# Attention heads loaded by four transfers per half instead of twelve, with a source that repeats, and a split spread over later steps of the rotated pass

## What is computed

```python
q, k, v = heads(x @ Wq + bq), heads(x @ Wk + bk), heads(x @ Wv + bv)   # 16 heads of 8
# second attention: q, k = rope(q), rope(k)
attn = softmax(q @ k.T / sqrt(8))          # 512 x 512 for each head
x = x + (attn @ v) @ Wo + bo
```

## Time and profile before

| | |
|---|---|
| median of 3 runs | 4861.33 us (4853.15 to 4867.28) |
| profiled execution: time, span | 4843.5 us, 4841.7 us |
| TensorE busy | 4504.4 us, 93% |
| VectorE (DVE) busy | 3527.2 us, 73% |
| ScalarE (ACT) busy | 2281.7 us, 47% |
| GpSimd (POOL) busy | 2492.3 us, 51% |
| transfers a_ks<-a_scr, a_qs<-a_scr | 96 of 192 KB, 288 of 64 KB |
| transfers a_scr<-a_parts | 48 of 256 KB |
| mean granted TensorE clock | 0.945 of full speed |

### The profile page before, as it was taken

How to read it: one execution, slowest core, us unless ns; L and a number is a source line. 1 busy time by engine, 2 the same in 40 slices (tenths; PEclk the granted TensorE clock), 3 DMA queues, 4 the chain that set the end, 5 groups by cost and what they waited for, 6 DMA issues and landing times. The chain is left out here.

```text
span 4841.7 us, 116672 instructions
## 1 busy us (share of the span) xinstructions
PE 4504.4 (93%) x46192; PEld 2659.9 (55%) x46384; DVE 3527.2 (73%) x3728; ACT 2281.7 (47%) x3395; POOL 2492.3 (51%) x3501
## 2 busy tenths in 40 slices
PE   5999889999999999999999999999999998588897
PEld 2333356666666666666666666666666665222223
DVE  5777467777778777778778777777777875477763
ACT  1666544444444444444444444444444443046663
POOL 1111166666666666666566666666666663212212
PEclk6999989999999999999999999999999998689998
DMA  3222122222222222222222223222222222122210
GB/s 71 57 54 55 54 62 59 52 60 70 66 60 60 53 73 70 54 59 62 75 59 61 59 57 84 56 56 63 54 67 63 57 56 65 34 54 54 53 29 20
DMA packets 181498, 281.71 MB, mean 58 GB/s; under 512 B 58080, under 2 KB 79840, under 8 KB 175456
## 3 DMA queue, kind: packets, MB, share of 16 engines
q1 hardware_dynamic: 153664, 241.45, 20.9%
q10 hardware_dynamic: 27648, 37.79, 3.5%
HBM read 61.70 MB, written 17.56 MB: 16 GB/s over the span
## 5 line engine op out<-in xcount | busy, mean ns | idle before, releaser
L1015 DVE SCALAR_TENSOR_TENSOR x<-l_r,l_qkvec,l_tab 128x1024 f32<-128x1024 f32 x768 | 936.4, 1279 | 25.3 <-ACT l_sq L925 23.3
L503 DVE TENSOR_REDUCE a_nmax<-a_pair 128x2 f32<-128x1024 f32 x512 | 609.3, 1221 | 261.1 <-PE a_pair L585 261.0
L428 ACT ACTIVATE a_pt<-a_st 128x512 f32<-128x512 f32 x1024 | 542.7, 605 | 282.0 <-PE a_st L569 276.6
L860 POOL TENSOR_TENSOR l_ntmp<-l_seed 128x32 f32<-128x32 f32 (+1 forms) x480 | 111.0, 231 | 773.4 <-ACT l_seed L914 754.6
L893 POOL TENSOR_TENSOR l_p<-l_p,l_srec 128x1024 f32<-128x1024 f32 x192 | 365.3, 1902 | 248.9 <-DVE l_srec L1094 192.5
L887 POOL TENSOR_TENSOR l_u<-x 128x512 f32<-128x512 f32 x384 | 490.7, 1278 | 0.0
L888 POOL TENSOR_TENSOR l_u<-x 128x512 f32<-128x512 f32 x384 | 489.9, 1276 | 0.0
L1264 PE MATMUL l_r<-l_pbd,l_va 128*64 128x160 f32 (+1 forms) x6144 | 442.7, 297 | 13.8 <-DMA l_pbd<-l_pt 13.5
L975 ACT ACTIVATE l_p<-l_p 128x1024 f32<-128x1024 f32 x192 | 203.5, 1060 | 520.3 <-DVE l_p L1073 520.3
L1174 PE MATMUL l_r<-xs,l_wqkv 128*128 (+1 forms) x768 | 424.1, 658 | 25.8 <-DVEq L1082 23.1
L1264 PEld LDWEIGHTS l_r<-l_pbd,l_va 128*64 128x64 f32 x6144 | 396.7, 138 | 74.9 <-issue 74.9
(11 more groups left out here) (179 smaller groups left out, 7385.3 us busy)
## 6 DMA issues: line engine op xcount, KB each, us to landing
l_kbd<-l_kn SPq DMA_DIRECT2D x1536, 64.0 KB, 2.0
l_pbd<-l_pt SPq DMA_DIRECT2D x768, 64.0 KB
l_pbd<-l_pt ACTq DMA_DIRECT2D x576, 64.0 KB
a_ks<-a_scr SPq DMA_DIRECT2D x96, 192.0 KB
a_qs<-a_scr SPq DMA_DIRECT2D x288, 64.0 KB
a_scr<-a_parts SPq DMA_DIRECT2D x48, 256.0 KB, 2.5
l_pbd<-l_pt SPq DMA_DIRECT2D x192, 56.0 KB
l_wqkv<-in_wqkv SPq DMA_DIRECT2D x6, 1536.0 KB, 6.9
```

Source lines behind the costliest of these rows:

```text
L428: nc.scalar.activation(pt[n % 2][:, r, :], st[(4 * n + r + par) % 3][:], ACT.Exp, scale=SC).then_inc(exp_done, 1)
L503: nc.vector.tensor_reduce(out=nmax[:, n, 2 * i:2 * i + 2], in_=pair[i][:], op=ALU.max, axis=AX.X, negate=True).then_inc(pair_dve[i], 1)
L1015: last = nc.vector.scalar_tensor_tensor(out=t[a][:, 2 * half:2 * half + 2, :], in0=R[a][:, half, :].unsqueeze(1).to_broadcast([D, 2, T]), ...
```

## The change

`load_heads` issues four transfers per half. The source of each begins with a dimension of three copies (step zero): one transfer fills all 72 rows of `ks`, and one for each part of q fills 24 rows of `qs`. The bytes written into `ks` and `qs` are the same. The wait at `qs_full` counts 4 transfers instead of 12. In the rotated pass the fourth and fifth piece of the split stand at steps 10 and 11 instead of 9 and 9.

```diff
                     h = slice(8 * half, 8 * half + 8)
+                    sp.dma_start(ks[p][0:KROWS, h, :],
+                                 scratch[p][1].rearrange("j (e h) t -> (j e) h t", e=HD)[:, h, :].unsqueeze(0)
+                                 .to_broadcast([SPLIT, SPLIT * HD, 8, T])).then_inc(qs_full[half], 16)
                     for i in range(SPLIT):
                         r = i * SPLIT * HD
-                        sp.dma_start(ks[p][r:r + SPLIT * HD, h, :],
-                                     scratch[p][1].rearrange("j (e h) t -> (j e) h t", e=HD)[:, h, :]).then_inc(qs_full[half], 16)
-                        for j in range(SPLIT):
-                            r = (i * SPLIT + j) * HD
-                            sp.dma_start(qs[p][r:r + HD, h, :],
-                                         scratch[p][0, i].rearrange("(e h) t -> e h t", e=HD)[:, h, :]).then_inc(qs_full[half], 16)
+                        sp.dma_start(qs[p][r:r + SPLIT * HD, h, :],
+                                     scratch[p][0, i].rearrange("(e h) t -> e h t", e=HD)[:, h, :].unsqueeze(0)
+                                     .to_broadcast([SPLIT, HD, 8, T])).then_inc(qs_full[half], 16)
...
-                split_slots = (4, 5, 6, 7, 8) if rope is None else (8, 8, 9, 9, 9)
+                split_slots = (4, 5, 6, 7, 8) if rope is None else (8, 8, 9, 10, 11)
...
-                            pe.wait_ge(qs_full[half], seen.next(qs_full[half], SPLIT * (SPLIT + 1) * 16))
+                            pe.wait_ge(qs_full[half], seen.next(qs_full[half], (SPLIT + 1) * 16))
```

## The result

The changed kernel takes 5003.35 us (median of 6 runs, 4983.91 to 5019.1) against 4846.92 us of the kernel before (6 runs, 4831.57 to 4867.28): a ratio of 1.0322, 95% interval 1.0297 to 1.0347. It is 156 us slower at the median; the profiled executions are 140.4 us apart (4843.5 and 4983.9 us, spans 4841.7 and 4982.1). The profiled execution of the changed kernel is the shortest of its six, so some 16 us of the difference at the median are in no trace. The forecast was 96 us more, 4957 us, with a range of 4865 to 5085 us.

What follows compares the result with a forecast made beforehand. TensorE, busy 93% of the span, was taken as the bound, with head loads barely hidden. Waits of 13.8 and 60.9 us plus 21 us of clock, together 96, on 4861.3 gave 4957 us, range 4865 to 5085.

Steps and rivals of the forecast that it cites:

- Three engines: Head loads: with three copies leading the source pattern, three DMA engines work, each with 48 rows instead of 15.
- The time of a row: Head loads: 0.32 us per 8 KB row on three engines, so a load takes 17.9 us, 3.5 longer than 14.3.
- Rival 1: Head loads: three engines but slow rows; 0.48 us gives 5079 us (chance 0.17), 0.79 us about 5430 us (0.04).
- rivals 2 and 3: Head loads on twelve engines: rival 2, rows at 0.79 us, 4870 us (0.12); rival 3, at 0.32 us, 4838 us (0.09).
- low end of three values: Row time with three engines: low 0.32 us from a sixteen-engine transfer, middle 0.48, high 0.79; the low was taken.
- Issuing hidden: SP's issue of head loads: twelve transfers take some 4 us, four about 1.4 us; the saving is hidden, costed at nothing.
- nothing to gain from the spread: Rotated pass, step 9: no TensorE stall behind the three pieces; the 2.77 us gap behind step 8 stays, so nothing gained.
- The waits: TensorE waiting for later loads in both attention passes: 13.8 us more in the plain pass, 60.9 in the rotated one.
- The later split: Rotated pass: the last split piece, and the scratch writes behind it, come 4.9 us later; 4.7 at the first boundary.
- The clock: Half clock after boundary stops: 3 us in each of six steady rotated units and once in the plain pass, 21 us.
- The sum: Whole kernel: plain pass 13.8, rotated pass 60.9 and clock 21 us, together 96 us, 2.0% slower.
- the forecast's own range: Three engines at about 0.32 us: 4925 to 4995 us, row at 0.31 to 0.36, clock's 21 us or none; chance 0.58.

Runs made afterwards that it cites:

- kernel with the copies second: Changed kernel with the three copies as second dimension of k's source, q's rows not repeated inside a transfer, split 8, 8, 9, 9, 9: 4840.28 us, ratio 0.9982.
- split alone: Kernel before, twelve transfers kept, rotated pass split at 8, 8, 9, 10, 11 instead of 8, 8, 9, 9, 9: 4925.53 us, ratio 1.0162.
- kernel with the copies second and the early spread: Four transfers with the copies as second dimension, rotated split at 7, 8, 9, 9, 9: 4835.78 us, ratio 0.9956; repeated, 4838.40 us, ratio 0.9964.
- transfers alone: Changed kernel with its four transfers but the earlier rotated split 8, 8, 9, 9, 9: 4935.84 us, ratio 1.0184.
- kernel with the copies second and the late steps: Four transfers with the copies as second dimension, rotated split at 8, 8, 9, 10, 11: 4882.12 us, ratio 1.0067.
- units shown above: Three units of the kernel with the copies as second dimension and rotated split 7, 8, 9, 10, 11: 4864.71 us, ratio 1.0012.
- Taking the pair apart: Kernel before, twelve transfers, rotated split at 7, 8, 9, 9, 9, so no two pieces stand together at step 8: 4863.62 us, ratio 1.0013.

## Why the prediction was right, and where its terms were off

**Three engines: right.** The share is 0.19 to 0.20, 79 to 80 GB/s. The kernel with the copies second shows the cause: it is the outermost count, not the repetition. The Trainium skill, "DMA: Bandwidth & Descriptors", rules for kernel authors, has this for a leading zero-stride dimension; the trace of the changed kernel agrees, with 0.19.

**The time of a row: the number right, its reason not shown.** 0.32 us taken, 0.32 measured; 17.9 us for a load, predicted 17.9. Rival 1 (0.48 us) fell with that, rivals 2 and 3 with the share. I had taken the low end of three values because each engine would write a run of partitions of its own. The same reasoning gave 0.35 us for the kernel with the copies second, and 0.55 came. So part of this hit is luck.

**Issuing hidden, nothing to gain from the spread: right.** The stop behind step 8 is 16.6 us in six units before and after. Fewer issues by themselves won nothing: with the copies second there are four as well, and that kernel is not clearly faster.

**The waits: nearly right in the rotated pass, too low in the plain one.** Predicted 13.8 us in the plain pass and 60.9 in the rotated one, measured 20.6 and 66.9. In the plain pass the row load came 4.2 us later, not 3.5, and at the boundary for which I had 1.3 us TensorE's stop grew by 2.4, from 0.91 to 3.27. In the rotated pass the first load (3.6 us longer against 3.5) and the first boundary (8.1 against 8.2) came out; the six steady boundaries have 9.9 us more each, or 9.2 less the waits for ACT, where I had 8.2.

**The later split: under-sized.** I took 4.9 us later for the scratch writes, from a stretch at full clock. DVE in the changed kernel, the steps 9 to 11:

```profile
4593.57 1.23 DVE L503 TENSOR_REDUCE a_nmax<-a_pair 128x2 f32<-128x1024 f32 x1 [0.70 <-PE a_pair L585]
4594.71 0.69 DVE L496 CAST a_parts<-a_left 128x1024 bf16<-128x1024 f32 x1
4595.49 1.23 DVE L503 TENSOR_REDUCE a_nmax<-a_pair 128x2 f32<-128x1024 f32 x1
4598.75 1.22 DVE L503 TENSOR_REDUCE a_nmax<-a_pair 128x2 f32<-128x1024 f32 x1 [2.04 <-PE a_pair L585]
4599.89 1.22 DVE L498 TENSOR_TENSOR a_left<-a_left,a_parts 128x1024 f32<-128x1024 f32 x1
4601.02 1.22 DVE L503 TENSOR_REDUCE a_nmax<-a_pair 128x2 f32<-128x1024 f32 x1
4604.08 1.22 DVE L503 TENSOR_REDUCE a_nmax<-a_pair 128x2 f32<-128x1024 f32 x1 [1.84 <-PE a_pair L585]
4605.23 0.68 DVE L496 CAST a_parts<-a_left 128x1024 bf16<-128x1024 f32 x1
```

From the second maximum of step 9 to the end of the last piece it is 12.3 us in this unit; before it was 4440.74 - 4436.93 = 3.8 us. That is 8.5 us later. DVE waits about 2 us in each step for TensorE, whose clock over these steps is

```profile
4593.00:4603.00 10.00, 10.00 (x32) 2.23 (x32) 6.54 (x6) 4.34 (x8) 0.00 (x0) 0.53 0.02 5
```

that is, about half of full, 1.2 GHz. From unit to unit it differs: the six steady units have the scratch writes 8.7, 10.3, 13.0, 13.0, 13.0 and 10.3 us after the write of the maxima, against 4.5 to 4.9 before, so 6.9 us later on average. The split alone shows it too, with 10.1 to 13.0 us, and +79 us where the step and its clock gave 47.

The extra delay does not show in the waits, though. The six units above wait 11.0, 10.0, 10.4, 10.6, 10.2 and 10.1 us at their boundaries: the longest wait belongs to the earliest writes. At half clock TensorE itself is late as well, so I put that part of the delay down as busy time and not as a wait. For the wait I estimate instead that the last piece, two steps later, leaves TensorE two steps less to do before the boundary, 2 x 3.6 = 7.2 us by the pace of the earlier trace rows; the split alone shows 7.3 us more at a steady boundary on average, where I had 4.7. No run here tests that estimate by itself.

**The clock: the term that failed most.** I gave it 21 us, 3 us for each stop. The price came from one unit of the plain pass, which began with a stop of only 1.27 us for ACT; behind the boundaries with stops of 0.7 to 0.95 us the clock stayed at 1.00. So one case was taken for a rule. The passes say +9.9 and +27.8 us of busy TensorE, 38 us, of which only the 27.8 of the rotated pass (I had 18) are clear of the spread: the two executions of the kernel with the copies second and the early spread have 532.7 and 524.1 us of it in this pass, the four kernels with the steps 8, 8, 9, 10, 11 or with all rows on three engines 549.5 to 553.9. It does not follow the stops as I had it: the transfers alone, with 18 us more of waits in the rotated pass, had 30.4 us of added busy time, and the split alone, with 49 us more of waits, 26.3. The kernel with the copies second and the late steps had 26.1, with waits of under 3.2 us at the steady boundaries. Around a long stop the clock is half for all of 17 us:

```profile
4539.00:4556.00 17.00, 10.24 (x33) 2.90 (x33) 4.22 (x5) 4.35 (x8) 0.00 (x0) 0.50 0.19 79
```

but short stops cost as much in sum, and the late pieces of the split often fall into such time.

**The sum.** Waits 74.7 predicted, 87.5 measured; clock 21 predicted, 38 measured; together 96 and 126. The other 14 us of the profiled execution lie outside the attention passes and are not explained by the change. The direction, the mechanism and the range of 4865 to 5085 held. The point forecast did not: +96 against +140 in the profiled executions and +156 at the median. Nor did the forecast's own range, 4925 to 4995 us: 5003 lies above it, since it took the clock's 21 us for the most that the clock could cost. The terms that were too small are the clock (by 17 us in these executions, though two executions of the same code in the plain pass differ by 12.5 us) and the waits (by 13 us, about half in each pass).

**What stays open.** Why the added busy time of the rotated pass is 26 to 30 us whether its stops are short or long. Why the clock was 0.58 over the steps behind step 8 in two of the units shown above and 0.82 in a third of the same kernel. Taking the pair apart did not settle it, and no kernel here holds the clock fixed.

## What to carry to other kernels

Look at how many DMA engines a transfer runs on, and not at the number of transfers: fewer, larger transfers with the copy dimension outermost ran on three engines, and the same four transfers with the copies inside ran on twelve (a share of 0.74). Rows on the busiest engine are a first guess only, since a row took 0.32 to 0.79 us. If a load ends exactly when it is needed, as here (13.9 us of 13.9), look for the last work ahead of it before moving anything later: a move that looked like 4.9 us was up to 8.5, and cost 7.3 us of waiting at each boundary. When adding up waits, put down TensorE's slower clock as a term per pass, from its busy time, and not per stop; and compare that busy time with a pass whose code is the same, since two executions of the same plain pass differed by 12.5 us.

## What the runs showed of the hardware

The same 144 rows of 8 KB into the same 72 partitions took, per row, 0.79 us in the kernel before while a share of 0.51 (eight engines) was at work, 0.55 us with the copies second at a share of 0.74 (twelve engines), and 0.32 us in the changed kernel at 0.19 (three engines). So three engines moved 79 GB/s where eight moved 85. If an engine takes neighbouring rows of a transfer, which no trace here shows, it writes one partition of eight in the first case, runs of three to six in the second, and runs of 8 and 24 in the third. That the crowding at the destination is the cause is argued from these three, not shown: the order in the source and the number of engines at work differ with them. The number of engines alone is not it, since a row takes 0.55 us with twelve, 0.76 us with twelve in the kernel before, and 0.32 us with sixteen in another transfer of it.
